# First products of the experts in a soft mixture: two blocks at a time, with fifth passes of 64 rows side by side

## The reference, cut to what matters

```python
logits = jnp.einsum('bnd,esd->bnes', x, phi)
dispatch = jax.nn.softmax(logits, axis=1)
combine = jax.nn.softmax(logits.reshape(B, N, E * S), axis=-1).reshape(B, N, E, S)
slots = jnp.einsum('bnd,bnes->besd', x, dispatch)
h = jax.nn.gelu(jnp.einsum('besd,edh->besh', slots, w1) + b1[None, :, None, :])
y = jnp.einsum('besh,ehd->besd', h, w2) + b2[None, :, None, :]
out = jnp.einsum('besd,bnes->bnd', y, combine)
```

## Time and profile before

| what | value |
|---|---|
| median of three runs | 929.48 us (921.3 to 929.79) |
| the profiled execution | 930.86 us, span 929.2 us |
| TensorE's mean granted clock | 0.979 |
| busy: PE, PEld, DVE, ACT, POOL | 93%, 75%, 49%, 49%, 19% of the span |
| first products of the experts (L221 with `wx`) | 480 matmuls, 116.2 us busy |
| second products (L1548) | 768 matmuls, 127.4 us busy |

### The profile page before, as it was taken

How to read it: one execution, slowest core, us unless ns; L and a number is a source line. 1 busy time by engine, 2 the same in 40 slices (tenths; PEclk the granted TensorE clock), 3 DMA queues, 4 the chain that set the end, 5 groups by cost and what they waited for, 6 DMA issues and landing times.

```text
span 929.2 us, 14911 instructions
## 1 busy us (share of the span) xinstructions
PE 864.3 (93%) x5408; PEld 693.0 (75%) x5408; DVE 459.4 (49%) x1025; ACT 459.9 (49%) x937; POOL 180.3 (19%) x257
## 2 busy tenths in 40 slices
PE   2899989989989899999998899999999899998998
PEld 1766866866766678878887579975989579984998
DVE  4878778688678633455553630164103640154001
ACT  5887677677677343244443443453233433443232
POOL 3040040040100122245200430035000340025000
PEclk9999989999999799999998999999999999999999
DMA  7010010000000000001003000000000000000000
GB/s 199 1 39 3 0 36 2 0 23 11 0 1 1 26 15 19 12 24 46 13 1 119 0 1 1 1 18 0 0 0 17 0 0 0 0 17 1 1 1 18
DMA packets 12712, 15.50 MB, mean 17 GB/s; under 512 B 5313, under 2 KB 10561, under 8 KB 12545
## 3 DMA queue, kind: packets, MB, share of 16 engines
q1 hardware_dynamic: 10656, 9.46, 3.3%
q0 software_dynamic: 2016, 5.51, 2.1%
HBM read 13.39 MB, written 1.57 MB: 16 GB/s over the span
## 4 chain that ended last, share of the span: by engine, by line
PE 77%; DVE 11%; ACT 5%; issue 5%; DMA 1%; SPq 0%; POOL 0%; DVEq 0%; ACTq 0%; POOLq 0%
PE ps L221 20%; PE ps L1548 13%; PE ps L1475 6%; PE ps L1203 6%; PE ps L1563 5%; PE ps L1121 4%; PE ps L1295 4%; PE ps L1101 3%; DVE area L275 2%; PE ps L1109 2%; PE ps L1333 1%; PE ps L1081 1%; DVE dstat L771 1%; ACT area L911 1%; PE ps L1161 1%
## 5 line engine op out<-in xcount | busy, mean ns | idle before, releaser
L221 PE MATMUL ps<-xs,ws 128*128 128x512 f32 x460 | 128.8, 426 | 5.5 <-DVE xs L502 3.7
L1548 PE MATMUL ps<-area 128*128 128x192 f32 x768 | 127.4, 326 | 0.0
L1548 PEld LDWEIGHTS ps<-area 128*128 128x128 f32 x768 | 124.8, 190 | 2.0 <-issue 0.5
L221 PE MATMUL ps<-ws,wx 128*128 128x512 f32 x480 | 116.2, 397 | 1.3 <-DVE ws L792 1.3
L1049 ACT ACTIVATE area<-ps,bcol 128x512 f32<-128x512 f32 x96 | 65.7, 689 | 86.6 <-PE ps L221 86.6
L221 PEld LDWEIGHTS ps<-xs,ws 128*128 128x128 f32 x460 | 88.7, 202 | 24.9 <-issue 6.6
L221 PEld LDWEIGHTS ps<-ws,wx 128*128 128x128 f32 x480 | 89.2, 188 | 22.8 <-DVE ws L792 3.0
L803 DVE TENSOR_TENSOR area<-ps,area 128x384 f32<-128x384 f32 x32 | 17.9, 559 | 177.8 <-PE ps L1548 177.8
L911 ACT ACTIVATE area<-ps,nm 112x196 f32<-112x196 f32 (+1 forms) x240 | 85.7, 441 | 18.8 <-DVE nm L637 18.8
L414 POOL TENSOR_TENSOR area<-area,dstat 128x512 f32<-128x512 f32 x32 | 33.0, 1042 | 276.6 <-DVE dstat L768 276.6
L637 DVE TENSOR_REDUCE nm<-ps 112x4 f32<-112x784 f32 (+1 forms) x72 | 62.9, 874 | 31.4 <-PE ps L1101 26.4
(11 more groups left out here) (179 smaller groups left out, 1403.5 us busy)
## 6 DMA issues: line engine op xcount, KB each, us to landing
stage<-in_wall POOLq DMA_DIRECT2D x42, 128.0 KB, 2.4
area<-in_w2e SPq DMA_DIRECT2D x1, 2304.0 KB, 8.3
out<-xres SPq DMA_DIRECT2D x4, 384.0 KB, 2.6
xres<-in_x SPq DMA_DIRECT2D x1, 1152.0 KB, 7.8
area<-in_wall SPq DMA_DIRECT2D x2, 512.0 KB, 5.6
area<-in_w2a SPq DMA_DIRECT2D x1, 576.0 KB, 3.7
room<-in_rel SPq DMA_DIRECT2D x4, 128.0 KB, 5.3
xres<-in_x SPq DMA_DIRECT2D x1, 384.0 KB, 3.1
```

What stands on the lines that cost most here:

```text
L221: last = mm(out_, l, r, start=n == 0, stop=n == len(pairs) - 1)
L1548: last = mm(ps[:, 4 + b, s * D:s * D + D], hTd[:, m, b * T + s * P:b * T + s * P + P], w2x[:, e * MC + m, :], start=m == 0, stop=m == MC - 1)
```

## The change

Three things change, in the experts' first products and in the copies that feed them.

- `slots_again` is a new name for columns of `ws[:, 3]`, free by then. After L1039 (now L1040) ScalarE copies rows 64 to 127 of the same bank a second time, into `slots_again` (L1042), and `d_sh` is raised after that. There are four such copies for each `it`.
- Blocks go in pairs (`m` and `m + 1`). Passes one to four of both blocks come first, eight full passes. Then the two fifth passes follow, each with 64 rows: block `m` with rows 0 to 63 of `wx[:, 3]` and `slots[2]`, block `m + 1` with rows 64 to 127 of `wx[:, 3]` and `slots_again`. They go to different banks. The product of the two low parts is left out by this.
- `d_gelu` is waited for once for each pair. The second product no longer waits at its start; its first six matmuls wait for the GELU of block `m` from `m` = 2 on. `gated` raises a semaphore of TensorE's own, which nobody waits for.

```diff
+        slots_again = ws[:, 3, 0:NE * 2 * NS]
...
                         A.activation(slot_cols(slots[2], b, h), ps[:, bank + 1, :].rearrange("p (e s) -> p e s", e=2),
-                                     ACT.Copy).then_inc(d_sh, 1)
+                                     ACT.Copy)
+                        A.activation(slot_cols(slots_again, b, h)[R1:P],
+                                     ps[R1:P, bank + 1, :].rearrange("p (e s) -> p e s", e=2), ACT.Copy).then_inc(d_sh, 1)
...
+                def hidden(e, m):
+                    if e == 0 and m == 2:
+                        pe.wait_ge(d_ss, 1 + it * 4 + 4)
+                        gated(pe, 0)
+                    c0, c1 = 512 * e, 512 * e + 512
+                    pe.wait_ge(d_gelu, 1 + it * NE * MC + max(0, e * MC + m - 2))
+                    gated(pe, 0)
+                    for n in range(2):
+                        bank, at = ps[:, (e * MC + m + n) % 4, :], (e * MC + m + n) * P
+                        for w_, x_ in ((0, 0), (1, 0), (0, 1), (2, 2)):
+                            mm(bank, wx[:, w_, at:at + P], slots[x_][:, c0:c1], start=w_ + x_ == 0, stop=False)
+                    for n, rows in enumerate((slice(0, R1), slice(R1, P))):
+                        bank, at = ps[:, (e * MC + m + n) % 4, :], (e * MC + m + n) * P
+                        x_ = slots_again if n else slots[2]
+                        mm(bank, wx[rows, 3, at:at + P], x_[rows, c0:c1], start=False, stop=True).then_inc(d_h, 1)
...
-                        pe.wait_ge(d_gelu, 1 + it * NE * MC + max(0, e * MC + m - 3))
-                        product(ps[:, (e * MC + m) % 4, :], (CW1 + (e * MC + m) * P, CW1 + (e * MC + m) * P + P),
-                                scols(512 * e, 512 * e + 512)).then_inc(d_h, 1)
-                    pe.wait_ge(d_gelu, 1 + it * NE * MC + e * MC + MC - 1)
+                    for m in range(0, MC, 2):
+                        hidden(e, m)
...
-                                if b + s == 0 and m == MC - 1:
-                                    pe.wait_ge(d_gelu, 1 + it * NE * MC + e * MC + MC)
+                                if b + s == 0 and m >= 2:
+                                    pe.wait_ge(d_gelu, 1 + it * NE * MC + e * MC + m + 1)
+                                    gated(pe, 0)
```

More of the change, by code:

```diff
@@ L1530, in body_d @@
                 pe.wait_ge(d_ss, 1 + it * 4 + 2)
-                for e in range(NE):
-                    for m in range(MC):
-                        if e == 0 and m == 2:
-                            pe.wait_ge(d_ss, 1 + it * 4 + 4)
-                        pe.wait_ge(d_gelu, 1 + it * NE * MC + max(0, e * MC + m - 3))
-                        product(ps[:, (e * MC + m) % 4, :], (CW1 + (e * MC + m) * P, CW1 + (e * MC + m) * P + P),
-                                scols(512 * e, 512 * e + 512)).then_inc(d_h, 1)
-                    pe.wait_ge(d_gelu, 1 + it * NE * MC + e * MC + MC - 1)
+                def hidden(e, m):
[13 more added lines that the diff above has]
+                        mm(bank, wx[rows, 3, at:at + P], x_[rows, c0:c1], start=False, stop=True).then_inc(d_h, 1)
+                for e in range(NE):
+                    for m in range(0, MC, 2):
+                        hidden(e, m)
                     pe.wait_ge(d_ye, 1 + it * 2 * NE + 2 * e)
```

## The result

The changed kernel took 940.54 us, the median of 6 runs (932.74 to 942.01), against 928.99 us for the kernel before in 6 runs (921.3 to 929.79). The ratio on record is 1.0131, with a 95% interval of 1.0095 to 1.0168 (the two medians alone give 1.0124): it is slower, by a little more than 1%. The profiled execution took 942.01 us, its span 940.3 us.

A forecast was written before the change was run, and what follows sets the result against it. TensorE, busy for 93% of the span, was taken to bound the kernel; +8.4 us for pairs and +2.0 us for the third copy, +10.4 us on 929.48, gave 939.9 us, with 930 to 945 us expected 8 times in 10.

The forecast's parts named there:

- two 64-row passes overlap: In each pair's fifth passes, the two 64-row passes run side by side, saving one pass of 0.228 us.
- one change of shape: On TensorE, each switch between full and 64-row passes costs 0.21 us: about 0.10 drain, about 0.11 weight load.
- net price of a pair: In the experts' first products, two changes of shape less one saved pass: +0.19 us a pair.
- 44 pairs: Of 48 pairs, the first of each it hides ahead of the slots wait; 44 at 0.19 us add +8.4 us.
- third copy, four times: ScalarE's extra copy delays the subtractions and TensorE's third block by 0.49 us, four times: +2.0 us, bounds 0 and 2.4.
- TensorE's release behind it: In TensorE's queue, gated and register instructions were put at nothing; the slots wait was to reach about 0.8 us.
- waits on GELU in the second product: At an expert's end, both last GELUs finish in time with 0.36 us in hand, so they cost nothing.
- clock in the mixture: TensorE's granted clock share stays at 1.00 in the mixture.
- Saving without a price: Rival for the pairs: the pass is saved and changes of shape cost nothing, 921.4 us; chance 6%.
- drains alone: Rival for the pairs: only the drains cost, weight loads being fetched ahead, 930.3 us; chance 10%.
- Passes in series: Rival for the pairs: the two 64-row passes run one after the other, 0.228 us more a pair, 949.9 us; chance 6%.
- The wait on GELU: Rival at the second product: late GELUs stop TensorE 16 times, 0.3 us each, adding 4.8 us, 944.7 us; chance 6%.

The follow-up runs named there:

- e3: Changed kernel with both 64-row passes of a pair on the same half, rows 0 to 63, third copy made but not read; median 945.48 us, ratio 1.0226.
- e1: Changed kernel with both fifth passes of a pair full (128 rows) again, pairs, waits and third copy kept; median 932.42 us, ratio 1.0062 to the kernel before.
- e2: Kernel before with only the third copy added ahead of d_sh, read by nothing; median 925.52 us, ratio 1.0007, mixture 406.59 us.
- e4: Changed kernel with d_sh raised ahead of the third copy, whose own semaphore VectorE awaits only before its second subtraction; median 937.53 us, ratio 1.0116.
- e5: Changed kernel without the d_gelu wait and its gated at the first expert's second pair; one profile, mixture 415.11 us, 0.6 less than the changed kernel.
- e7: Changed kernel with ScalarE's copies reordered: slots[2] first, slots[0] second, third copy last; one profile, 1.73 us from first copy to subtraction, mixture 415.67 us.
- e9: Changed kernel with the third copy over all 128 rows; one profile, 1.61 us from first copy to subtraction, mixture 415.19 us.
- e6: Kernel before, but experts two to four run six 64-row passes first in one stretch, third copy beside the first subtraction; median 927.04 us, ratio 0.9995.

## Why the prediction was right, step by step

The forecast was 939.9 us and the way slower; 940.54 was measured. In the mixture, where the clock is the same, +10.4 us were forecast and +11.5 measured. That the times agree within 0.7 us is in part luck: the difference was 1.1 us short, the forecast started from 929.48 where the six runs before gave 928.99, and runs of one kernel spread over 9 us. The difference and its terms are what the mechanism has to answer for.

| step | forecast | measured |
|---|---|---|
| two 64-row passes overlap | yes | yes: 0.43 us for both, 0.66 in one half (e3) |
| one change of shape | 0.21 us | 0.40 for two |
| net price of a pair | +0.19 us | +0.18 to 0.19 (e1: 8.0 / 44, or 8.2 / 44 without the stray step; chain: 0.56 / 3) |
| 44 pairs | +8.4 us | +8.0 to 8.2 |
| third copy, four times | +2.0 us | +2.4 (e2, e4) |
| TensorE's release behind it | nothing | +1.0 (4 x 0.24; 0.6 of it undone by e5) |
| waits on GELU in the second product | none | none: no such row among TensorE's waits |
| clock in the mixture | 1.00 | 1.00 |

**The pairs** were sized from rows of other forms: full f32r passes beside 64-column ones, and plain f32 passes of 64 rows. The f32r passes of 64 rows paid the same. The first pair of each turn stays hidden, as forecast: in e3, with one pass more ahead of TensorE's wait for the slots, that wait falls from 4.7 to 3.8 us. The rule of the Trainium skill that spoke against the change (TensorEngine Tiling (Array Packing), Tiling Modes: changing the tiling mode drains the array) held, and the trace shows more than a drain: of 0.20 us for one change, about half (0.11, the step behind the first pass in a new shape) goes with a weight load that no longer runs under the pass ahead. The trace agrees with the Trainium skill's rule for tiles side by side (TensorE: Matmul & The Clock Gate, Part 3) for the two passes among themselves, which start 3 to 4 ns apart; the rule leaves out the edges, and the 921.6 us that it alone would give are 19 us off.

**The third copy** was mis-sized: I took 0.49 us, the step between two copies of 128 rows, and read from the earlier trace rows that fewer rows cost no less. They cost more: 0.60, the bound that I had put above. The copy starts only after the one ahead has ended. By e7 that is not the bank's doing, and e9 with the four lines beside it ties it to the first row, 64 behind 0. What rows 9 give is the time of one operation, and the term needed the step from one to the next.

**The release** was left out: I put `gated` and register instructions at nothing because a stream of passes with register instructions in it holds its pace. That is so while TensorE's queue runs ahead of the array: e1's second products, with four `gated` each, hold 7.80 us. Where TensorE stands at a wait, whatever is queued behind it comes after the release, and there two waits with `gated` took 0.24 us more than the two waits without it in the kernel before. So TensorE's wait grew from 0.3 to 1.2 us a turn and not to 0.8.

Together the copy and the release were 1.4 us short and the pairs 0.2 to 0.4 us over, so the mixture's forecast was about 1 us low. In the chain I had looked for 7.4 us of first products; 7.19 stand there, because the last drain and load of an expert fall into L1564's 8.00. Two figures of the working are a little off and change nothing: L1475's passes start 0.43 us apart (7.12 / 16 = 0.445 takes in the run-out of the last one), and a pair at 0.21 gives 940.7 us, not 940.9.

**The rivals.** Saving without a price, and drains alone, are out by e1 (8.0 us come back with the full passes). Passes in series are out by e3. The wait on GELU did not come with the late waits of the changed kernel; with the early wait of the kernel before and shorter blocks (e6) it did.

What stays open: how the time after a release divides between a wait and the `gated` behind it. The kernel before has two waits and no `gated` in that place and a gap of 0.04, and the trace shows each `gated` in the gap, which speaks for `gated`; the changed kernel with both waits and no `gated` was not tried. Why an operation of ScalarE at another first row starts late, and e1's one gap of 0.44 us, stay open too.

## What to carry to other kernels

In this kernel two matmuls over half of the rows each run side by side in the time of one, but going to that shape and back costs about 0.4 us, nearly two passes of 512 columns (0.228 us each). Count passes saved for each stretch in the other shape, not for each pair: here one pair to a stretch loses 0.18 us, three gain 0.27. When a stage gets shorter, look which wait behind it was nearly late already.

## What the runs showed of the hardware

- ScalarE starts an operation before the one ahead has ended: 0.49 us after its start where both cover 128 rows and each lasts 0.60. The Trainium skill has that (ScalarE: Activation LUTs, What ACT_TABLE_LOAD costs: back-to-back ACTIVATEs overlap by about 93 ns), and the trace agrees, with about 0.11 us. Where the next operation began at another row it waited for the end instead: rows 64 to 127 behind 128 rows started 0.60 us after the start, so a copy of fewer rows took longer. Rows 0 to 63 behind 128 rows kept the overlap (L984 behind L983, 0.1 us).
- Behind a wait, TensorE takes 0.28 us to its next matmul with two waits and their `gated` in the queue, 0.14 with one, 0.04 with two waits and no `gated`.
